# Reordering the first eight sequences of a gather-and-matmul kernel (ramp order on five queues)

## The chip, the cores and the metric

The kernel runs on one core of one Trainium2 chip. The metric is the device time of one execution in microseconds (us), the median of three runs.

## What is computed

64 sequences of 128 rows by 512 columns pass through two steps, each added to its input:

```python
attn_in = tanh(x @ W1 + b1); scores = attn_in @ v
p = softmax(where(mask_of_kind, scores, -1e30))      # prefix, postfix or cloze mask, one kind per sequence
x = x + (p @ x) / cnt
x = x + (x @ W[cat] + b[cat])                        # W[cat] is 512x512 float32, gathered per sequence
```

The kernel multiplies out the second step: with W' = W + identity it forms y = x W', and then out = y + p' y + b, where p' is p divided by cnt.

## The kernel before

Four sequences form a group g (16 groups). For each group one x tile of 1 MB is loaded and for each sequence k one W tile of 1 MB. In the steady part every float32 operand is split into a high and a low float32r half, and three products replace one float32 product. The work of one sequence is spread over the engines like this:

- SyncE (SP) issues nearly all loads and all stores. It runs through a list written by hand: the opening loads, then a loop over t with a store, now and then an x or a bias row, and the next W.
- VectorE (DVE) adds the identity to W (`add_identity`, 0.6 us), forms the low halves (`split_w_lo`, `split_xT_lo`, `split_z_lo`, `split_mix_lo`, `split_av_lo`), the row maxima (`max_group`) and every fourth output (`add_wide`).
- ScalarE (ACT) forms the high halves (`split_w_hi`, `split_xT_hi`, `split_z_hi`, `split_mix_hi`), tanh, exp, the scaling of the probabilities (`scale_group`) and three of four outputs (`copy_out`).
- GpSimd (POOL) adds the identity for two of four sequences and multiplies the row sums (`row_div`), and copies masks.
- TensorE (PE) runs `xw(k)` (12 products), `pz(k-2)` (3 or 4), and once per group `transpose_probs(g)`, `hidden(g+1)` (12) and `scores_group(g+1)` (2). Group 0 uses unsplit float32 (`xw_raw`, `hidden_raw`).

Every engine works strictly in the order of its program and waits on semaphores. From sequence 7 on (8 after the change) the order comes from loops. Before that, in the ramp, it is written out line by line, and the change touches this part. W buffers: 5 raw, 4 high, 3 low. `split_z_hi(3)` needs `pz(0)` done, since there are three z buffers. Below, w5 is the W tile of sequence 5, id5 its identity addition, x1 the x tile of group 1, T1 the transposes of group 1.

Of the kernel before, what the change touches and what calls it, by code (L numbers as in the profile page):

```python
# [38 lines left out]
def program(nc, xg, ids, w1, w, bias, out):  # L40
    GROUPS, P, DC, GS = xg.shape
# [14 lines left out]
    with ctx:  # L56
# [265 lines left out]
        def _(act):  # L322
# [70 lines left out]
            split_z_hi(1)
            split_w_hi(4)
            split_z_hi(2)
            split_mix_hi(0)
            tanh_group(1)
# [343 lines left out]
```

## Time and profile before

| | us |
|---|---|
| median of 3 runs | 311.19 (310.75 to 311.24) |
| profiled execution, its own time | 310.89 |
| its span | 308.9 |
| PE busy | 299.9 (97%) |
| DVE busy | 281.9 (91%) |
| ACT busy | 266.6 (86%) |
| POOL busy | 90.1 (29%) |

The page of the profile gives busy time by engine, a chain that ended last, and groups of instructions. The rows that matter here are single instructions of the first 61 us, in order of time, with what each had waited for.

### The profile page before, as it was taken

How to read it: one execution, taken by the hardware profiler on the slowest of the kernel's cores; microseconds unless marked ns; L12 is line 12 of the kernel's file. 1: busy time of each engine (PE TensorE's matmuls, PEld its weight loads, DVE VectorE, ACT ScalarE, POOL GpSimd, SP SyncE). 2: the span in 40 equal slices, each digit the busy share in tenths (PEclk: the TensorE clock that was granted, in tenths of full speed). 3: DMA queues.
4: the chain of work that ended last, by engine and by line, in shares of the span. 5: the costliest groups of instructions: out<-in, count | busy, mean ns of one | idle time of the engine just before them, and what ended most of it. 6: DMA issues, size and time to landing. Idle time of an engine off the chain costs nothing.

```text
span 308.9 us, 4918 instructions
## 1 busy us (share of the span) xinstructions
PE 299.9 (97%) x1292; PEld 233.8 (76%) x1292; DVE 281.9 (91%) x383; ACT 266.6 (86%) x431; POOL 90.1 (29%) x123
## 2 busy tenths in 40 slices
PE   7999899899999999999999999999999999999995
PEld 4444686688787878878788887878888787888884
DVE  4459889999999999999999999999999999999961
ACT  2287988989999998999999899998989999899952
POOL 4011612334142243414224341322434132302100
PEclk9999999999999999999999999999999999999999
DMA  7999999999999999999999999999999999997243
GB/s 265 366 426 366 421 412 423 371 344 326 360 372 332 396 313 405 356 356 375 337 404 300 407 363 363 365 337 398 311 405 355 353 380 308 413 333 228 66 135 137
DMA packets 23516, 105.69 MB, mean 342 GB/s; under 512 B 2625, under 2 KB 2626, under 8 KB 13378
## 3 DMA queue, kind: packets, MB, share of 16 engines
q1 hardware_dynamic: 23202, 104.08, 90.6%
q10 hardware_dynamic: 288, 1.31, 1.1%
q8 instruction: 10, 0.16, 0.2%
q14 instruction: 16, 0.13, 0.1%
HBM read 88.61 MB, written 16.78 MB: 341 GB/s over the span
## 4 chain that ended last, share of the span: by engine, by line
PE 82%; DMA 6%; issue 5%; DVE 3%; ACT 1%; POOL 1%; ACTq 0%; POOLq 0%; SPq 0%; DVEq 0%
PE ps_y L653 16%; PE ps_y L655 16%; PE ps_y L654 16%; PE ps_pre L615 12%; DMA w_raw<-in_L_cond_W 6%; PE ps_y L665 4%; PE ps_y L666 4%; PE ps_y L667 4%; PE ps_y L671 3%; PE ps_pT L632 2%; PE ps_y L641 1%; PE ps_scores L625 1%; PE ps_scores L623 1%; POOL w_raw L274 1%; DVE w_lo L465 1%
## 5 line engine op out<-in xcount | busy, mean ns | idle before, releaser
L465 DVE TENSOR_TENSOR w_lo<-w_raw,w_hi 128x2048 fp32r<-128x2048 f32 x60 | 140.1, 2335 | 0.0
L336 ACT ACTIVATE w_hi<-w_raw 128x2048 fp32r<-128x2048 f32 x60 | 115.5, 1924 | 8.9 <-POOL w_raw L274 7.5
L653 PE MATMUL ps_y<-w_hi,xT_hi 128*128 128x512 f32 x240 | 95.0, 396 | 0.0
L655 PE MATMUL ps_y<-w_hi,xT_lo 128*128 128x512 f32 x240 | 93.6, 390 | 0.0
L654 PE MATMUL ps_y<-w_lo,xT_hi 128*128 128x512 f32 x240 | 93.4, 389 | 0.0
L274 POOL TENSOR_TENSOR w_raw<-w_raw,ident 128x512 f32<-128x512 f32 x30 | 39.2, 1307 | 132.6 <-DVE w_lo L465 82.6
L655 PEld LDWEIGHTS ps_y<-w_hi,xT_lo 128*128 128x128 f32 x240 | 45.0, 188 | 9.8
L654 PEld LDWEIGHTS ps_y<-w_lo,xT_hi 128*128 128x128 f32 x240 | 45.1, 188 | 9.1
L653 PEld LDWEIGHTS ps_y<-w_hi,xT_hi 128*128 128x128 f32 x240 | 45.1, 188 | 8.9 <-issue 0.2
L493 DVE TENSOR_TENSOR z_lo<-ps_y,z_hi 128x512 fp32r<-128x512 f32 x64 | 43.5, 680 | 5.4 <-ACT z_hi L372 5.3
L372 ACT ACTIVATE z_hi<-ps_y 128x512 fp32r<-128x512 f32 x64 | 38.7, 604 | 7.8 <-PE ps_y L655 5.1
L281 POOL COPY mask<-penalty 128x128 bf16 x64 | 42.5, 695 | 9.8 <-issue 9.7
L458 DVE TENSOR_TENSOR xT_lo<-x_raw,xT_hi 128x2048 fp32r<-128x2048 f32 x15 | 34.2, 2281 | 0.0
L378 ACT ACTIVATE out_sb<-ps_y 128x512 f32<-128x512 f32 x48 | 28.9, 603 | 2.0 <-PE ps_y L671 2.0
L327 ACT ACTIVATE xT_hi<-x_raw 128x2048 fp32r<-128x2048 f32 x15 | 28.8, 1923 | 0.0
L453 DVE TENSOR_TENSOR w_raw<-w_raw,ident 128x512 f32<-128x512 f32 x33 | 22.5, 682 | 4.4 <-DMA w_raw<-in_L_cond_W 4.4
L665 PE MATMUL ps_y<-z_hi,mix_hi 128*128 128x512 f32 x64 | 25.2, 394 | 0.9 <-DVE z_lo L493 0.7
L666 PE MATMUL ps_y<-z_hi,mix_lo 128*128 128x512 f32 x64 | 24.9, 389 | 0.0
L667 PE MATMUL ps_y<-z_lo,mix_hi 128*128 128x512 f32 x64 | 24.9, 389 | 0.0
L351 ACT ACTIVATE probs<-ps_scores,neg_max 128x128 f32<-128x128 f32 x64 | 22.3, 359 | 2.0 <-DVE neg_max L478 2.0
L615 PE MATMUL ps_pre<-xT_hi,w_hi 128*128 128x512 f32 x56 | 22.9, 409 | 0.6 <-issue 0.6
L316 POOL TENSOR_TENSOR row_div<-row_sum,seen 128x4 f32<-128x4 f32 x16 | 6.4, 401 | 56.8 <-ACT probs L351 56.8
(70 smaller groups left out, 352.8 us busy)
## 6 DMA issues: line engine op xcount, KB each, us to landing
w_raw<-in_L_cond_W SPq DMA_DIRECT2D x63, 1024.0 KB, 8.6
out<-out_sb SPq DMA_DIRECT2D x64, 256.0 KB, 6.2
x_raw<-in_x SPq DMA_DIRECT2D x15, 1024.0 KB, 7.4
out_sb<-in_L_cond_b SPq DMA_DIRECT2D x16, 256.0 KB, 5.7
x_raw<-in_x SPq DMA_DIRECT2D x2, 512.0 KB, 4.8
w_raw<-in_L_cond_W ACTq DMA_DIRECT2D x1, 1024.0 KB, 6.1
w_pack<-in_W_b_v ACTq DMA_DIRECT2D x1, 257.0 KB, 2.9
b_raw<-in_L_cond_b SPq DMA_DIRECT2D x2, 128.0 KB, 12.9
```

The source lines that it names most:

```text
L274: nc.gpsimd.tensor_tensor(blocks, blocks, eye, ALU.add).then_inc(pool_wi_ready, 1)
L281: last = nc.gpsimd.tensor_copy(mask[g % 2][:, i:i + 1, :], penalty[:, bass.ds(kind, 1), :])
L336: nc.scalar.activation(w_hi[k % NH][:], w_raw[k % NW][:], ACT.Copy).then_inc(w_hi_ready, 1)
L372: nc.scalar.activation(z_hi[k % NZ][:], ps_y[k % NY][:], ACT.Copy).then_inc(z_hi_ready, 1)
L465: nc.vector.tensor_tensor(w_lo[k % NL][:], w_raw[k % NW][:], w_hi[k % NH][:].bitcast(F32), ALU.subtract).then_inc(w_lo_ready, 1)
L493: nc.vector.tensor_tensor(z_lo[k % NZ][:], ps_y[k % NY][:], z_hi[k % NZ][:].bitcast(F32), ALU.subtract).then_inc(z_lo_ready, 1)
L615: last = nc.tensor.matmul(ps_pre[:], wp[:, c, :], xp[g % NT][:, c, :], start=(c == 0 and i == 0), stop=(c == DC - 1 and i == 2))
L653: nc.tensor.matmul(y[:], xT_hi[q][:, c, xs], w_hi[k % NH][:, c, :], start=(c == 0), stop=False)
L654: nc.tensor.matmul(y[:], xT_hi[q][:, c, xs], w_lo[k % NL][:, c, :], start=False, stop=False)
L655: last = nc.tensor.matmul(y[:], xT_lo[q][:, c, xs], w_hi[k % NH][:, c, :], start=False, stop=(c == DC - 1))
L665: nc.tensor.matmul(y[:], mh, z_hi[k % NZ][:], start=False, stop=False, skip_group_check=True)
L666: nc.tensor.matmul(y[:], ml, z_hi[k % NZ][:], start=False, stop=False, skip_group_check=True)
```

## The change

- **Loads.** w1 moves from SP to ScalarE's queue, right behind w0. SP no longer waits for the second half of x0 but for w0 to land, then issues w2, w4, x1, w3, the bias table (two halves, `b_raw`), w5, x2, w6, a bias row, w7, w8, w9, x3. Before: w1, w2, x1, w4, w3, w5, bias table, x2, w6, bias row, w7, w8, and x3 only after the first store.
- **id3** is done by POOL, not DVE.
- **PE** runs the transposes of group 1 after `xw(5)` and `pz(3)`, not after `xw(4)` and `pz(2)`.
- **ACT and DVE** get another order for sequences 1 to 7, and the written-out part is one sequence longer.

```diff
-            return {3: 6, 4: 5}.get(k, k + 2 - pool_count(k - 1))
+            return k + 2 - pool_count(k - 1)
...
-            return k > G and k % G in (1, 2)
+            return k == 3 or k > G and k % G in (1, 2)
...
             sp.wait_ge(ids_in, 16)
-            sp.wait_ge(x0_in[1], 16)
-            load_w(1)
-            load_w(2)
+            cat_2 = load_cat(2)
+            sp.wait_ge(w_in[0], 16)
+            load_w(2, cat_2)
+            load_w(4)
             load_x(1)
-            load_w(4)
             load_w(3)
-            load_w(5)
             sp.dma_start(b_raw[0:C, :], bias).then_inc(b_low_in, 16)
             sp.dma_start(b_raw[C:P, :], bias).then_inc(b_high_in, 16)
+            load_w(5)
             load_x(2)
             load_w(6)
             load_wide(0)
+            load_w(7)
+            load_w(8)
+            load_w(9)
+            load_x(3)
...
             for g in range(GROUPS):
+                if g == 1:
+                    add_identity(3)
...
-            cat_0 = act.value_load(ids_row[0:1, 0:1], min_val=0, max_val=C - 1)
-            act.dma_start(w_raw[0][:], w[bass.ds(cat_0, 1)].rearrange("a p c h -> p (a c) h")).then_inc(w_in[0], 16)
+            for k in range(2):
+                cat = act.value_load(ids_row[0:1, k:k + 1], min_val=0, max_val=C - 1)
+                act.dma_start(w_raw[k][:], w[bass.ds(cat, 1)].rearrange("a p c h -> p (a c) h")).then_inc(w_in[k], 16)
...
-                if k < B and b == 0:
+                if k < B and (k == G + 1 or b == 0 and g >= 2):
                     transpose_probs(g)
```

First place: DVE from id4 (the second row of that kind here, `w_raw<-w_raw,ident`) to the maxima of group 1. Before:

```order
30 L484 RECIPROCAL row_scale<-row_div 128x4
31 L453 TENSOR_TENSOR w_raw<-w_raw,ident 128x4x128
32 L458 TENSOR_TENSOR xT_lo<-x_raw,xT_hi 128x2048
33 L453 TENSOR_TENSOR w_raw<-w_raw,ident 128x4x128
34 L465 TENSOR_TENSOR w_lo<-w_raw,w_hi 128x2048
35 L493 TENSOR_TENSOR z_lo<-ps_y,z_hi 128x512
36 L488 TENSOR_TENSOR mix_lo<-ps_pT,mix_hi 128x512
37 L470 SCALAR_TENSOR_TENSOR av_lo<-attn,w_pack,av_hi 128x512
38 L554 TENSOR_TENSOR b_both<-b_raw,b_both 64x512
39 L493 TENSOR_TENSOR z_lo<-ps_y,z_hi 128x512
```

The same stretch of the changed kernel (its lines are numbered otherwise):

```order
30 L502 RECIPROCAL row_scale<-row_div 128x4
31 L471 TENSOR_TENSOR w_raw<-w_raw,ident 128x4x128
32 L483 TENSOR_TENSOR w_lo<-w_raw,w_hi 128x2048
33 L506 TENSOR_TENSOR mix_lo<-ps_pT,mix_hi 128x512
34 L511 TENSOR_TENSOR z_lo<-ps_y,z_hi 128x512
35 L569 TENSOR_TENSOR b_both<-b_raw,b_both 64x512
36 L488 SCALAR_TENSOR_TENSOR av_lo<-attn,w_pack,av_hi 128x512
37 L476 TENSOR_TENSOR xT_lo<-x_raw,xT_hi 128x2048
38 L496 ISA ps_scores,neg_max<-ps_scores,mask 128x128
39 L496 ISA neg_max 128x1
```

The low half of x1 went from the front of the stretch to its end, behind av_lo of group 1; id3 is gone; z_lo of sequence 2 went behind the maxima.

Second place: ACT from the tanh of group 2 on. Before:

```order
35 L342 ACTIVATE attn<-ps_pre,w_pack 128x512
36 L344 ACTIVATE av_hi<-attn,w_pack 128x512
37 L378 ACTIVATE out_sb<-ps_y 128x512
38 L336 ACTIVATE w_hi<-w_raw 128x2048
39 L372 ACTIVATE z_hi<-ps_y 128x512
40 L336 ACTIVATE w_hi<-w_raw 128x2048
41 L351 ACTIVATE probs,row_sum<-ps_scores,neg_max 128x128 x4
42 L378 ACTIVATE out_sb<-ps_y 128x512
43 L372 ACTIVATE z_hi<-ps_y 128x512
44 L358 ACTIVATE probs<-probs,row_scale 128x128 x4
```

And in the changed kernel:

```order
39 L355 ACTIVATE attn<-ps_pre,w_pack 128x512
40 L357 ACTIVATE av_hi<-attn,w_pack 128x512
41 L391 ACTIVATE out_sb<-ps_y 128x512
42 L349 ACTIVATE w_hi<-w_raw 128x2048
43 L385 ACTIVATE z_hi<-ps_y 128x512
44 L391 ACTIVATE out_sb<-ps_y 128x512
45 L364 ACTIVATE probs,row_sum<-ps_scores,neg_max 128x128 x4
46 L349 ACTIVATE w_hi<-w_raw 128x2048
47 L385 ACTIVATE z_hi<-ps_y 128x512
48 L371 ACTIVATE probs<-probs,row_scale 128x128 x4
```

The high half of w10 (the second `w_hi` row) went behind the exp of group 2, between it and the scaling.

## Rows read from the trace of the kernel before

**Rows 1.** The page: the busy line of the engines.

```profile
PE 299.9 (97%) x1292; PEld 233.8 (76%) x1292; DVE 281.9 (91%) x383; ACT 266.6 (86%) x431; POOL 90.1 (29%) x123
```

**Rows 2.** Timeline, TensorE: start, length, engine, line, operation, waited before.

```profile
13.83 7.03 PE L641 MATMUL ps_y<-w_raw,x_raw 128*128 128x512 f32 x16
...
28.36 0.19 PEld L625 LDWEIGHTS ps_scores<-av_lo,ones 128*128 128x128 f32 x1 [0.59 <-DVE av_lo L470]
29.08 0.19 PEld L665 LDWEIGHTS ps_y<-z_hi,mix_hi 128*128 128x128 f32 x1 [0.54 <-DVE b_both L554]
...
35.79 0.66 PE L632 MATMUL ps_pT<-ident,probs 128*128 128x128 f32 x4 [1.19 <-ACT probs L358]
...
53.99 0.50 PE L665 MATMUL ps_y<-z_hi,mix_hi 128*128 128x512 f32 x1 [0.68 <-DVE z_lo L493]
...
55.99 0.66 PE L632 MATMUL ps_pT<-ident,probs 128*128 128x128 f32 x4 [0.80 <-ACT probs L358]
...
60.93 0.47 PE L615 MATMUL ps_pre<-xT_hi,w_hi 128*128 128x512 f32 x1 [0.62 <-issue]
```

**Rows 3.** Critical chain, in order of time: two later transposes, and two loads.

```profile
3.14 6.12 DMA w_raw<-in_L_cond_W
...
13.70 12.71 DMA w_raw<-in_L_cond_W
...
75.06 0.44 PE ps_pT L632 x4
...
93.19 0.44 PE ps_pT L632 x4
```

**Rows 4.** Timeline, VectorE: identities, low halves, and one reciprocal.

```profile
12.73 0.69 DVE L453 TENSOR_TENSOR w_raw<-w_raw,ident 128x512 f32<-128x512 f32 x1 [1.16 <-DMA w_raw<-in_L_cond_W]
...
20.28 0.69 DVE L453 TENSOR_TENSOR w_raw<-w_raw,ident 128x512 f32<-128x512 f32 x1 [3.05 <-DMA w_raw<-in_L_cond_W]
...
27.20 1.10 DVE L470 SCALAR_TENSOR_TENSOR av_lo<-attn,w_pack,av_hi 128x512 fp32r<-128x512 f32 x1
...
30.62 2.28 DVE L465 TENSOR_TENSOR w_lo<-w_raw,w_hi 128x2048 fp32r<-128x2048 f32 x1
34.24 0.18 DVE L484 RECIPROCAL row_scale<-row_div 128x4 f32<-128x4 f32 x1 [1.34 <-POOL row_div L316]
...
38.31 2.28 DVE L465 TENSOR_TENSOR w_lo<-w_raw,w_hi 128x2048 fp32r<-128x2048 f32 x1
...
45.71 0.87 DVE L470 SCALAR_TENSOR_TENSOR av_lo<-attn,w_pack,av_hi 128x512 fp32r<-128x512 f32 x1 [1.12 <-ACT av_hi L344]
...
47.10 3.07 DVE L465 TENSOR_TENSOR w_lo<-w_raw,w_hi 128x2048 fp32r<-128x2048 f32 x1
...
54.45 0.17 DVE L484 RECIPROCAL row_scale<-row_div 128x4 f32<-128x4 f32 x1
```

**Rows 5.** Timeline, GpSimd: its first three identities that met VectorE.

```profile
26.48 1.27 POOL L274 TENSOR_TENSOR w_raw<-w_raw,ident 128x512 f32<-128x512 f32 x1 [6.32 <-DMA w_raw<-in_L_cond_W]
32.32 1.73 POOL L274 TENSOR_TENSOR w_raw<-w_raw,ident 128x512 f32<-128x512 f32 x1 [4.57 <-DMA w_raw<-in_L_cond_W]
...
46.72 1.30 POOL L274 TENSOR_TENSOR w_raw<-w_raw,ident 128x512 f32<-128x512 f32 x1 [0.69 <-DMA w_raw<-in_L_cond_W]
```

**Rows 6.** DMA view: throughput in 40 slices of 0 to 62 us, then of 20 to 32 us.

```profile
GB/s 0 226 256 412 439 233 328 418 423 428 428 428 428 423 428 373 248 367 423 398 437 423 418 418 423 390 403 433 398 437 403 443 410 414 440 363 392 354 370 383
...
GB/s 410 437 437 410 410 437 410 437 437 410 437 410 437 437 273 341 191 328 225 273 259 294 300 382 355 437 437 410 410 437 437 382 437 410 437 437 280 376 539 410
```

**Rows 7.** Timeline, ScalarE: one high half, av_hi, the output after exp(2), scaling(2).

```profile
18.45 1.89 ACT L327 ACTIVATE xT_hi<-x_raw 128x2048 fp32r<-128x2048 f32 x1
...
25.49 0.72 ACT L344 ACTIVATE av_hi<-attn,w_pack 128x512 fp32r<-128x512 f32 x1
...
52.60 0.61 ACT L378 ACTIVATE out_sb<-ps_y 128x512 f32<-128x512 f32 x1
...
54.66 1.28 ACT L358 ACTIVATE probs<-probs,row_scale 128x128 f32<-128x128 f32 x4 [0.96 <-DVE row_scale L484]
```

More of the change, by code:

```diff
@@ L228, in load_wide @@
             def load_wide(g):
-                cat = sp.value_load(ids_row[0:1, G * g + WIDE:G * g + WIDE + 1], min_val=0, max_val=C - 1)
+                cat = load_cat(G * g + WIDE)
                 if g >= 1:
@@ L249, in _ @@
             load_wide(0)
-            for t in range(B + 3):
+            load_w(7)
+            load_w(8)
+            load_w(9)
+            load_x(3)
+            for t in range(3, B + 3):
                 g, b = t // G, t % G
-                if t >= 3:
-                    store(t - 3)
-                if b == 3 and g + 3 < GROUPS:
+                store(t - 3)
+                if b == 3 and 1 <= g < GROUPS - 3:
                     load_x(g + 3)
-                if b == 2 and 1 <= g < GROUPS:
+                if b == 2 and g < GROUPS:
                     load_wide(g)
@@ L391, in _ @@
             scale_group(0)
+            split_w_hi(4)
+            split_z_hi(1)
+            split_mix_hi(0)
             split_xT_hi(1)
[L393 to L397, printed above, removed]
             act.wait_ge(b_low_in, 16)
@@ L400, in _ @@
             nc.scalar.activation(b_both[:], b_raw[:], ACT.Copy).then_inc(b_hi_ready, 1)
+            tanh_group(1)
+            split_z_hi(2)
             split_w_hi(5)
+            split_z_hi(3)
             split_xT_hi(2)
+            copy_out(0)
             exp_group(1)
-            split_z_hi(3)
-            copy_out(0)
+            split_w_hi(6)
             scale_group(1)
-            split_w_hi(6)
+            split_z_hi(4)
+            split_w_hi(7)
             split_mix_hi(1)
-            split_z_hi(4)
+            split_z_hi(5)
             copy_out(2)
-            split_w_hi(7)
-            split_z_hi(5)
             split_w_hi(8)
@@ L416, in _ @@
             split_w_hi(9)
-            for k in range(G + 3, B + 3):
+            split_z_hi(6)
+            copy_out(4)
+            exp_group(2)
+            split_w_hi(10)
+            for k in range(2 * G, B + 3):
                 g, b = k // G, k % G
@@ L555, in _ @@
                 .then_inc(bias_ready, 1)
+            split_av_lo(1)
+            split_xT_lo(1)
+            max_group(1)
             split_z_lo(2)
-            max_group(1)
             split_w_lo(5)
+            split_z_lo(3)
+            split_xT_lo(2)
             row_scale_group(1)
-            split_xT_lo(2)
-            split_z_lo(3)
+            add_wide(0)
             add_identity(7)
-            add_wide(0)
             split_w_lo(6)
+            split_z_lo(4)
             split_mix_lo(1)
-            split_z_lo(4)
             add_identity(8)
@@ L571, in _ @@
             split_w_lo(8)
-            for k in range(G + 3, B + 1):
+            max_group(2)
+            split_w_lo(9)
+            row_scale_group(2)
+            split_z_lo(6)
+            add_identity(11)
+            for k in range(2 * G, B + 1):
                 g, b = k // G, k % G
@@ L638, in xw_raw @@
                         pe.wait_ge(wi_ready, c // HALF + 1)
+                    elif c == 0 and by_pool(k):
+                        pe.wait_ge(pool_wi_ready, pool_count(k))
                     elif k >= 1 and c == 0:
```

14 lines of the change are left out of this document (7 added, 7 removed).

## The prediction

> **What bounds the kernel now.** I read the page first. PE is busy for 97% of the span, DVE for 91%, and the page's chain lies on PE almost throughout [rows 1]. So ask where PE waits. The timeline of PE shows it waiting only in the first 61 us [rows 2]; after that the transposes come every 18.13 us (75.06, then 93.19) [rows 3] and nothing interrupts PE. The change ends at sequence 8, so its worth is the shift of the moment at which PE falls into that rhythm, which I read at the transposes of group 3, 75.06.
>
> PE's waits on the way are: low half of av 0.59 at 28.36, bias 0.54 at 29.08, T1 1.19 at 35.79, pz(6) 0.68 at 53.99, T2 0.80 at 55.99, hidden(3) 0.62 at 60.93 [rows 2]. That looks like 4.4 us to win. But every one of them ends with DVE's or ACT's work, and from 20.28 on DVE waits for others only 1.34 us at 34.24, 1.12 before the av_lo of group 2, and behind POOL (below) [rows 4]. DVE is the engine that is late. Whatever lets DVE start a long piece earlier is worth time; what only reorders PE is not.
>
> **The change part by part.**
>
> *w1 behind w0 on ACT's queue.* w0 lands at 3.14 + 6.12 = 9.26 [rows 3]. w1 landed at about 12.7, since its identity waited for it until 12.73 [rows 4]; the throughput falls to 233 and 328 GB/s between 7.8 and 10.9 us against some 425 around it [rows 6]. With w1 already queued, (425 - 233 + 425 - 328) x 1.55 us is 0.45 MB, or 1.05 us of the stream. But PE reaches xw(1) only at 13.83 and runs it and xw(2) without a gap [rows 2], so w1 early is worth nothing by itself. w2 is now issued after w0 has landed, 9.3, and should land 4.9 later, as w1 did after its issue at 7.8: 14.2. From there 1.05 MB at 425 GB/s is 2.5 us each.
>
> *Order of loads.* w4 comes at 16.7 (before: 20.2, where id4 waited for it [rows 4]), x1 at 19.2. From w4's landing to w6's at 32.2 the kernel before took 12.0 us for w3, w5, bias table, x2 and w6 [rows 4, 5]. At 2.5 each and 0.6 for the table that is 10.6. The rest went in a dip to 191 to 382 GB/s from 24.2 to 27.5 us [rows 6], which begins as the bias table moves. The same five loads follow x1 now. If the dip goes with the table, w6 lands at 19.2 + 12.0 = 31.2 and w5 two loads earlier, 26.2, against 26.41 before (13.70 + 12.71 [rows 3]); if not, 1.2 us or so earlier: 30.0 and 25.0. I take the dip as tied to the table, since it is the only one in the first 54 us. So of the stream's lead of 1.05 us, w5 keeps 0.2 and w6 1.0.
>
> *id3 to POOL.* DVE saves 0.6 us (0.69 in the row, of which the next operation overlaps some 0.08, as with all of DVE's here: 0.6 for an identity or a z, 2.2 for a w or xT low half [rows 4]). POOL is idle there; w3 lands at 21.7, id3 takes 1.3 [rows 5] and is done at 23.0, while PE is still in hidden_raw(1), whose tanh comes just ahead of av_hi at 25.49 [rows 7]. No cost for PE.
>
> *DVE, first place.* w_hi(4) now follows scale_group(0) at 18.45 (where xT_hi(1) stood [rows 7]), so w_lo(4) runs 20.35 to 22.55, then mix_lo(0) and z_lo(1) to 23.75. Now DVE waits: 0.65 for b_both (behind xT_hi(1), 21.9 to 23.7 on ACT, and 0.6 long), and, after its 0.6, 1.2 for av_hi(1). That one can't move: it starts at 25.49 + 0.76 = 26.25 [rows 7], fixed by PE's float32 products. So 1.9 us of DVE are lost here, which before held xT_lo(1).
> Then POOL. An identity on POOL and a DVE operation on two SBUF tiles don't run together: av_lo at 27.20 took 1.10 instead of 0.75 until just after id5's end at 27.75, w_lo at 47.10 took 3.07 instead of 2.28 while POOL's lasted to 48.02, and id6 at 32.32 took 1.73 instead of 1.27 behind the w_lo that ended at 32.90 [rows 4, 5]. Now id5 runs 26.3 to 27.5, so av_lo(1) ends at 28.0 instead of 27.0. xT_lo(1) takes 2.2 to 30.2, the maxima 1.0 to 31.2, z_lo(2) 0.6 to 31.8. w6 has landed at 31.2 and id6 runs until 32.5, so w_lo(5) ends at 34.65 (0.7 lost; before, id6 fell into a moment in which DVE had nothing to do). z_lo(3), xT_lo(2), row_scale, add_wide(0), id7: 0.6 + 2.2 + 0.1 + 0.6 + 0.6, and w_lo(6) starts at 38.75, against 38.31 [rows 4]. **+0.45.** The wait of 1.34 at 34.24 is gone, and so is id3, but 1.9 + 1.0 + 0.7 of new waits took their place.
>
> *T1 one sequence on.* PE: the waits at 28.36 and 29.08 fall away, since b_both and mix_lo(0) are early, and pz(0) starts some 0.6 sooner; xw(5) waits for w_lo(5) until 34.7, ends at 37.4, pz(3) at 38.4; scale_group(1) follows row_scale at 37.5 and ends at 38.8, so T1 waits only 0.4. PE has done more by then, but mix_hi(1) waits for T1 and ACT's w_hi(7), and id8 on DVE comes after mix_lo(1): w_lo(6) to 40.95, z_lo(4), mix_lo(1), id8 to 42.75, against 42.31. w_hi(8), tanh(2), av_lo, w_lo(8) and the maxima of group 2 then follow as before, av_lo waiting for av_hi as at 45.71 and w_lo(8) for POOL as at 47.10 [rows 4]. Nothing is gained or lost: still +0.45.
>
> *ACT, second place.* Before, exp(2) ended at 52.60; two short copies followed, and ACT waited 0.96 for row_scale(2), which came at 54.45 [rows 4, 7]. Now row_scale(2) comes 0.8 earlier, right behind w_lo(9), but w_hi(10) stands ahead of scale_group(2): exp to 53.05, w_hi(10) 1.8, z_hi(7) 0.5, scaling 1.2 (1.28 in the row [rows 7]), T2 at about 56.7 against 55.99. For DVE, row_div(2) (which waits for w_lo(9) on POOL, too), then z_lo(6) and id11, then w_lo(10) at 55.4 and xT_lo(3), which ends at about 61.6; hidden(3) waits for it: 0.3 to 0.4 more. **Together +0.8.** Bounds of this part: 0, if ACT's gap of 0.96 takes up most of w_hi(10), and 0.7 (T2's own shift).
>
> *Later loads* (w7, w8, w9, x3 before the first store): w8 still waits for xw(3), and w9 lands before its identity, which waits for w_lo(7). The first store waits for nothing new. I cost it at nothing: before, PE had no wait for a load there, and x3 comes earlier.
>
> Sum: 75.06 + 0.8. The profiled execution took 310.89, so 311.7; the median shown is 0.3 above it, 311.19, so 312.0. I take 311.9, since each lock of POOL and DVE was priced in full.
>
> **A rule beside the rows.** By the rows above two of those waits cost 1.7 us in the first place; without them the sum would be +0.8 - 1.7 = -0.9. The Trainium skill, page "SBUF — State Buffer", section "SBUF: two separate sides", says that DVE and GpSimd share a port pair by an exclusive lock, that a DVE operation with two SBUF inputs takes part in it, and that the loser blocks wholly. By that rule moving id3 to POOL gains only where DVE is not at such an operation, and the three rows agree with it.
>
> **The rivals.**
> - *No dip.* If the dip at 24 to 27 us was chance and doesn't follow the bias table, w5 lands at 25.0, before av_lo(1) is due, and w6 at 30.0, so id6 is done by 31.3. av_lo ends at 27.0, w_lo(6) starts at 37.5 (-0.8), and with the +0.4 of the second place, which stays, the shift is -0.4: 310.8. For it: a load of bias rows at 31 us made no such dip. Against it: the dip starts with the table's rows.
> - *The waits are won after all (the other side).* If POOL's identities cost DVE nothing, its pieces from 26.25 to w_lo(6) add up to 0.75 + 2.2 + 1.0 + 0.6 + 2.2 + 0.6 + 2.2 + 0.1 + 0.6 + 0.6 = 10.85, so w_lo(6) starts at 37.1, 1.2 early; and if row_scale(2) ahead of z_lo(6) gives back half of T2's wait of 0.80 [rows 2], another 0.4: 1.6 in all, 309.6 to 310.3. It decides from the point at which w5 has landed and been treated by POOL before 26.3 and w6 before 30.8. Against it: three rows of POOL against DVE [rows 4, 5].
> - *The stream is later.* w2 goes out after w0's landing, with nothing of SP's queued, and if the first packets are slow again or w5 comes after 26.7, av_lo, xT_lo(1) and w_lo(5) are pushed 0.5 further: +1.3 to +1.5, 312.5.
> - *Nothing at all.* The change takes a PE wait here and makes one there. Terms of +0.45 and +0.35, each good to some 0.3, may come to nothing: 311.2. This is the low end of the forecast case.
>
> **How the numbers follow.** Dip with the table (my forecast, own range +0.2 to +1.2): 0.5. No dip: 0.23. Won after all: 0.15. Later stream: 0.12. A difference under 0.2% (0.62 us) can't be told from none here. The forecast case splits into 0.29 slower and 0.21 same; no dip into 0.15 same and 0.08 faster; won is faster; later is slower. Faster 0.08 + 0.15 = 0.23; same 0.21 + 0.15 = 0.36; slower 0.29 + 0.12 = 0.41. Range: from the middle between "no dip" and "won", 310.2, to 312.8.
>
> **What would show it.** w1 landing by 11.8 and w2 by 14.3 in their waits; DVE idle about 1.9 us between 23.7 and 26.3; the second w_lo (w5's) of over 2.9 us; w_lo(6) at 38.5 to 39; T1 waiting under 0.5; T2 waiting 1 us behind w_hi(10); group 3's transposes at 75.6 to 76. The prediction is wrong if w5 lands before 25.3, or if DVE's slots behind POOL are short.

## The result, and the profile after

The changed kernel is slower: median 313.08 us (312.46 to 315.45, 11 runs) against 311.19 (310.67 to 312.95, 11 runs) of the kernel before, run beside it; ratio 1.0063, interval 1.0044 to 1.0082. That is 1.9 us, above the 311.9 that was forecast and above the range's upper end, 312.8. Repeated (after_again below) the ratio was 1.0044. The ratios here and below are those on record with their 95% intervals; they are not quotients of the two medians, and where the two differ enough to matter the text says so.

The page of the profiled execution: its span is 310.5 (before 308.9), and the busy line answers to [rows 1].

```profile
span 310.5 us, 4917 instructions
...
PE 301.8 (97%) x1292; PEld 234.2 (75%) x1292; DVE 282.9 (91%) x382; ACT 266.7 (86%) x431; POOL 93.2 (30%) x124
```

The chain that ended last, in order of time (start, length, what), over the ramp and the first regular groups:

```profile
13.20 11.39 DMA b_raw<-in_L_cond_b
24.72 0.49 issue
25.22 0.68 ACT attn L355
25.92 0.73 ACT av_hi L357
...
27.35 3.36 DVE xT_lo L476
...
57.48 0.66 PE ps_pT L654 x4
...
76.52 0.44 PE ps_pT L654 x4
...
94.67 0.44 PE ps_pT L654 x4
```

Group 3's transposes are at 76.52 instead of 75.06 [rows 3], 1.46 late, and the next come 18.15 later, as before. So the loss is made in the ramp. Where the chain before had the W tile of sequence 5 (13.70 12.71 [rows 3]) it now has the bias table: ScalarE forms b_both from it ahead of tanh of group 1, so tanh waits for the table, then comes av_hi, and behind that VectorE's low half of x1.

VectorE's timeline, the pieces that answer to [rows 4]:

```profile
17.61 0.69 DVE L471 TENSOR_TENSOR w_raw<-w_raw,ident 128x512 f32<-128x512 f32 x1 [0.42 <-DMA w_raw<-in_L_cond_W]
20.33 2.29 DVE L483 TENSOR_TENSOR w_lo<-w_raw,w_hi 128x2048 fp32r<-128x2048 f32 x1 [2.03 <-ACT w_hi L349]
...
25.34 0.69 DVE L569 TENSOR_TENSOR b_both<-b_raw,b_both 64x512 fp32r<-64x512 f32 x1 [1.52 <-ACT b_both L412]
26.68 0.75 DVE L488 SCALAR_TENSOR_TENSOR av_lo<-attn,w_pack,av_hi 128x512 fp32r<-128x512 f32 x1 [0.64 <-ACT av_hi L357]
27.35 3.36 DVE L476 TENSOR_TENSOR xT_lo<-x_raw,xT_hi 128x2048 fp32r<-128x2048 f32 x1
...
32.19 3.17 DVE L483 TENSOR_TENSOR w_lo<-w_raw,w_hi 128x2048 fp32r<-128x2048 f32 x1
...
38.08 0.17 DVE L502 RECIPROCAL row_scale<-row_div 128x4 f32<-128x4 f32 x1
...
39.34 2.28 DVE L483 TENSOR_TENSOR w_lo<-w_raw,w_hi 128x2048 fp32r<-128x2048 f32 x1
...
42.36 0.69 DVE L506 TENSOR_TENSOR mix_lo<-ps_pT,mix_hi 128x512 fp32r<-128x512 f32 x1
42.97 0.68 DVE L471 TENSOR_TENSOR w_raw<-w_raw,ident 128x512 f32<-128x512 f32 x1
...
54.67 0.18 DVE L502 RECIPROCAL row_scale<-row_div 128x4 f32<-128x4 f32 x1
...
55.95 2.38 DVE L483 TENSOR_TENSOR w_lo<-w_raw,w_hi 128x2048 fp32r<-128x2048 f32 x1
```

The wait of 3.05 for w4 is now 0.42, and the one of 1.34 for the row sums is gone. In their place stand 2.03, 1.52 and 0.64, and two low halves of 3.36 and 3.17 where 2.28 is the undisturbed length. GpSimd's timeline shows the identities that lie beside those two (26.93 and 31.91), and that both W tiles came later than forecast (26.2 and 31.2):

```profile
23.50 1.27 POOL L285 TENSOR_TENSOR w_raw<-w_raw,ident 128x512 f32<-128x512 f32 x1 [3.38 <-DMA w_raw<-in_L_cond_W]
26.93 1.63 POOL L285 TENSOR_TENSOR w_raw<-w_raw,ident 128x512 f32<-128x512 f32 x1 [2.16 <-DMA w_raw<-in_L_cond_W]
31.91 1.30 POOL L285 TENSOR_TENSOR w_raw<-w_raw,ident 128x512 f32<-128x512 f32 x1 [3.36 <-DMA w_raw<-in_L_cond_W]
...
54.06 0.58 POOL L329 TENSOR_TENSOR row_div<-row_sum,seen 128x4 f32<-128x4 f32 x1 [4.78 <-ACT probs L364]
```

ScalarE's timeline, b_both ahead of tanh, then the second place:

```profile
24.68 0.63 ACT L412 ACTIVATE b_both<-b_raw 128x512 fp32r<-128x512 f32 x1 [1.00 <-DMA b_raw<-in_L_cond_b]
25.22 0.67 ACT L355 ACTIVATE attn<-ps_pre,w_pack 128x512 f32<-128x512 f32 x1
25.92 0.72 ACT L357 ACTIVATE av_hi<-attn,w_pack 128x512 fp32r<-128x512 f32 x1
...
53.86 1.92 ACT L349 ACTIVATE w_hi<-w_raw 128x2048 fp32r<-128x2048 f32 x1
...
56.14 1.28 ACT L371 ACTIVATE probs<-probs,row_scale 128x128 f32<-128x128 f32 x4
```

And TensorE's waits, against [rows 2]:

```profile
30.85 0.47 PE L677 MATMUL ps_y<-w_hi,xT_hi 128*128 128x512 f32 x1 [0.26 <-DVE xT_lo L476]
35.50 0.47 PE L677 MATMUL ps_y<-w_hi,xT_hi 128*128 128x512 f32 x1 [0.74 <-DVE w_lo L483]
39.61 0.66 PE L654 MATMUL ps_pT<-ident,probs 128*128 128x128 f32 x4 [0.20 <-ACT probs L371]
...
55.48 0.50 PE L689 MATMUL ps_y<-z_hi,mix_hi 128*128 128x512 f32 x1 [0.93 <-DVE z_lo L511]
57.48 0.66 PE L654 MATMUL ps_pT<-ident,probs 128*128 128x128 f32 x4 [0.80 <-ACT probs L371]
62.42 0.47 PE L637 MATMUL ps_pre<-xT_hi,w_hi 128*128 128x512 f32 x1 [0.62 <-issue]
```

T1 hardly waits any more (0.20 for 1.19), yet it starts 3.8 us later: a sequence's products are ahead of it, as they should be, and with them a share of DVE's delay. Of the last three, pz(6) waits 0.93 for 0.68, T2 and hidden(3) as long as before, all of them 1.5 us later. These waits add up to less than those of [rows 2], so a list of TensorE's waits alone would not show the loss.

### The profile page after: what moved, and what is told of

It is laid out like the page before. It is cut to its first block, busy times and chain, and to the rows that moved or that the text cites. A ratio compares the mean times of both kernels' runs of the same rounds, so it can differ in the third digit from the quotient of the medians.

```text
span 310.5 us, 4917 instructions
## 1 busy us (share of the span) xinstructions
PE 301.8 (97%) x1292; PEld 234.2 (75%) x1292; DVE 282.9 (91%) x382; ACT 266.7 (86%) x431; POOL 93.2 (30%) x124
## 4 chain that ended last, share of the span: by engine, by line
PE 80%; DMA 6%; DVE 4%; issue 4%; ACT 4%; SPq 1%; ACTq 0%; DVEq 0%
PE ps_y L677 16%; PE ps_y L679 16%; PE ps_y L678 16%; PE ps_pre L637 12%; PE ps_y L689 4%; PE ps_y L690 4%; PE ps_y L691 4%; DMA b_raw<-in_L_cond_b 4%; PE ps_y L695 3%; PE ps_pT L654 2%; DMA w_raw<-in_L_cond_W 2%; DVE xT_lo L476 2%; DVE w_lo L483 1%; PE ps_scores L647 1%; PE ps_scores L645 1%
## 5 line engine op out<-in xcount | busy, mean ns | idle before, releaser
L285 POOL TENSOR_TENSOR w_raw<-w_raw,ident 128x512 f32<-128x512 f32 x31 | 40.5, 1307 | 130.2 <-DVE w_lo L483 82.2
L292 POOL COPY mask<-penalty 128x128 bf16 x64 | 43.8, 714 | 8.9 <-issue 8.8
L476 DVE TENSOR_TENSOR xT_lo<-x_raw,xT_hi 128x2048 fp32r<-128x2048 f32 x15 | 35.3, 2355 | 0.0
L371 ACT ACTIVATE probs<-probs,row_scale 128x128 f32<-128x128 f32 x64 | 20.7, 419 | 2.4 <-DVE row_scale L502 2.4
```

The lines of the kernel that those rows point to most:

```text
L285: nc.gpsimd.tensor_tensor(blocks, blocks, eye, ALU.add).then_inc(pool_wi_ready, 1)
L292: last = nc.gpsimd.tensor_copy(mask[g % 2][:, i:i + 1, :], penalty[:, bass.ds(kind, 1), :])
L476: nc.vector.tensor_tensor(xT_lo[g % NT][:], x_raw[g % NX][:], xT_hi[g % NT][:].bitcast(F32), ALU.subtract).then_inc(xT_lo_ready, 1)
```

## The experiments

Where an experiment's profile is read, T0 and T3 are the starts of the transposes of group 0 and group 3. Before they are 20.70 and 74.90, 54.20 apart; in the changed kernel 20.65 and 76.36, 55.71 apart, and in its repetition 54.73. (75.06 and 76.52 in the chain are within the same transposes, 0.16 behind their starts.) One profile's distance thus carries about 1 us of chance; the ratios of repeated runs decide.

The start of w_lo(6) on VectorE shows where that chance lies. From T0 to w_lo(6) the three profiles have 17.61, 18.69 and, in the repetition, 17.71: its T0 came 0.74 us later (21.39), while id5 ran 0.26 earlier (26.67), so the loads behind w0 did not move with T0. From w_lo(6) to T3 it is 36.59 before, 37.02 in the changed kernel and 37.02 again in its repetition. This second part is steady: 36.91 to 37.06 in the six variants of the changed kernel whose clock didn't fall (a1, a2, a4, c1, c2, d3), 36.32 to 36.73 in those of the kernel before. So of the 1.46 us, 1.03 lie ahead of w_lo(6) and 0.43 behind it.

**The changed kernel once more** (after_again), to have it beside the others.

> The changed kernel itself beside the others, to have its size on this chip: all theories expect the ratio of the first measurement again, 1.006, and the transposes of group 3 some 55.7 to 55.9 us after those of group 0.

312.61 us, ratio 1.0044 (1.0025 to 1.0063). The loss holds, at 1.0 us between the medians and 1.4 by the ratio.

### Parts taken back from the changed kernel

**tanh(1) ahead of b_both**, and on VectorE av_lo ahead of it:

```diff
             split_xT_hi(1)
+            tanh_group(1)
             act.wait_ge(b_low_in, 16)
             act.wait_ge(b_high_in, 16)
             nc.scalar.activation(b_both[:], b_raw[:], ACT.Copy).then_inc(b_hi_ready, 1)
-            tanh_group(1)
```

> The changed kernel (313.1 us median) with tanh(1) ahead of b_both on ScalarE and av_lo(1) ahead of the bias low half on VectorE. Theory A (b_both waited for the bias table until 24.68 and pushed tanh(1) from 24.77 to 25.22, av_lo(1) by 0.43): tanh(1) back at 24.8, av_lo(1) at 26.25; since POOL's id5 then blocks xT_lo(1) from 26.9 to 28.2 all the same, only 0.3 us comes back: 312.8. Theory B (the loss is in the late stream alone, w5 landing at 26.9): no change, 313.1. Theory C (the loss is T1's place on TensorE): no change.

312.79 us, ratio 1.0003 (0.9985 to 1.0020). The kernel before was at 312.36 beside this run and the next three, above its 311.2 to 311.6 everywhere else, and the changed kernel itself was not run there. So these four ratios don't say how much of the loss came back; the four are better compared with each other. The profile: VectorE waits for av_hi for 2.38 instead of for b_both and av_hi, and b_both, now beside GpSimd's identity, takes 1.65 instead of 0.69. T3 minus T0 is 55.72, w_lo(6) starts 18.66 after T0 (18.69 in the changed kernel). The wait changed its name.

**The bias table in one transfer** to 128 partitions (the table is given twice in DRAM):

```diff
-            sp.dma_start(b_raw[0:C, :], bias).then_inc(b_low_in, 16)
-            sp.dma_start(b_raw[C:P, :], bias).then_inc(b_high_in, 16)
+            sp.dma_start(b_raw[:], bias[0:P, :]).then_inc(b_low_in, 16)
```

> The changed kernel with the bias table loaded by one transfer into 128 partitions (the table stands twice in DRAM) instead of two into 64 each. Theory A (the dip in throughput comes from two transfers that each reach half of the partitions): no dip at 21 to 24 us, table at 23, w5 lands 1.2 us sooner at 25.7, w_lo(6) starts at 38.5 instead of 39.34, T3 0.9 to 1.2 sooner: 312.0. Rival (the dip comes from reading 64 rows of 2 KB in any shape, or by chance at that time): dip stays, 313.1.

311.92 us, ratio 0.9995 (0.9974 to 1.0016), T3 minus T0 55.04. The dip in throughput at the table was gone, w5 came 0.6 us earlier than in the changed kernel, w_lo(6) started at 38.75, 0.6 earlier too. The median is 0.8 to 1.2 us below those of the three other variants run beside it (312.79, 313.13, 312.70), which all keep the table in two transfers. So in the changed kernel the two transfers may well cost some of the loss. But the DMA view of this kernel (40 slices of 18 to 38 us) has another dip, at 29 to 31:

```profile
GB/s 475 344 475 344 492 459 287 455 442 430 467 360 492 426 377 459 426 410 459 344 508 459 279 209 168 311 430 401 430 426 426 393 459 377 459 442 410 426 459 393
```

**id3 back on VectorE**, behind z_lo(1):

```diff
-            return k == 3 or k > G and k % G in (1, 2)
+            return k > G and k % G in (1, 2)
...
             split_z_lo(1)
+            add_identity(3)
             dve.wait_ge(b_hi_ready, 1)
```

> The changed kernel with id3 back on VectorE, behind z_lo(1) at 23.7, where VectorE waits 1.5 us for b_both. Theory A (that wait hides it): 0 to +0.1 us, 313.1 to 313.2. Rival (VectorE is short of time everywhere in the ramp, so each 0.6 us of work counts): +0.6, 313.7.

313.13 us, ratio 1.0020 (1.0001 to 1.0039). In its profile TensorE's granted clock fell to 0.50 of full for some 3 us at 59 us (below), so its T3 isn't read. Up to w_lo(6) it is the changed kernel: VectorE had nothing to do where id3 went, and xT_lo(1) and w_lo(5) took 3.36 and 3.13, and w_lo(6) starts 18.93 after T0 for 18.69. Where id3 is done made no difference that shows.

**w_hi(10) ahead of exp(2)**, as in the kernel before:

```diff
-            copy_out(4)
-            exp_group(2)
             split_w_hi(10)
+            exp_group(2)
+            copy_out(4)
```

> The changed kernel with w_hi(10) ahead of exp(2) again, as in the kernel before. Theory A (w_hi(10) behind exp(2) cost 0.2 of T2, whose shift grew from 1.25 at w_lo(8) to 1.49): T2 at 57.2 instead of 57.48, 312.8. Rival (the second place cost 0.35 or more, as predicted): 312.7 or less; or nothing, if row_scale(2) is the limit: 313.1.

312.70 us, ratio 1.0012 (0.9990 to 1.0034). T2 doesn't wait any more, but hidden(3) does, for 1.64 instead of 0.62:

```profile
56.86 0.60 PE L654 MATMUL ps_pT<-ident,probs 128*128 128x128 f32 x4
62.77 0.47 PE L637 MATMUL ps_pre<-xT_hi,w_hi 128*128 128x512 f32 x1 [1.64 <-issue]
```

T2's wait of 0.8 was given back at hidden(3), which reads xT_lo(3), and from w_lo(6) to T3 it is 37.04, as in the changed kernel: at the second place VectorE's xT_lo(3) decides, not ScalarE's order.

**x1 ahead of w4 again** (loads, high and low halves):

```diff
-            load_w(4)
             load_x(1)
+            load_w(4)
...
-            split_w_hi(4)
+            split_xT_hi(1)
             split_z_hi(1)
+            split_w_hi(4)
             split_mix_hi(0)
-            split_xT_hi(1)
...
             add_identity(4)
+            split_xT_lo(1)
             split_w_lo(4)
```

> The changed kernel with x1 loaded ahead of w4 again, and both halves of x1 split ahead of w4's, where VectorE is otherwise idle. Theory A (the change lost its time by moving 2.2 us of VectorE work, xT_lo(1), out of an idle stretch into the busy one behind av_lo(1)): w_lo(6) at 37.9 instead of 39.3, group 3's transposes 1.0 to 1.4 us sooner counted from those of group 0, ratio to before 1.000 to 1.002. Rival (the loss is T1's place, id3 and the order at exp(2)): no change, 1.0045 to 1.006.

312.07 us, ratio 1.0030 (1.0001 to 1.0059); in its profile T3 minus T0 is 54.15, that of the kernel before. By the ratio half of the loss may be left, by the profile nothing: w_lo(6) starts 17.13 after T0, 0.5 less than before, which makes up for the 0.43 behind it. Here w_lo(4) meets id3 and takes 3.34, and id6, begun together with w_lo(5) (30.88), takes 3.44.

**id5 and id6 on VectorE** (and `by_pool`, the rule that says whose identity it is, with them):

```diff
             split_av_lo(1)
+            add_identity(5)
             split_xT_lo(1)
             max_group(1)
             split_z_lo(2)
+            add_identity(6)
             split_w_lo(5)
```

> The changed kernel with id5 and id6 on VectorE (1.2 us more work there, none on GpSimd between 24 and 43 us). Theory A (VectorE and GpSimd exclude each other, and each of GpSimd's two identities costs VectorE 0.7 to 1.1 us): w_lo(5) takes 2.3 instead of 2.9 to 3.2 us, xT_lo(1) or av_lo(1) isn't stretched, w_lo(6) starts at 38.5 to 39.2, the time is the same or 0.3 to 0.8 less, 1.002 to 1.005. Rival (the long operations had another reason): they stay long and 1.2 us of work comes on top, 1.010.

312.06 us, ratio 1.0027 (1.0006 to 1.0049). VectorE's timeline shows both low halves at their own length, each 0.6 of an identity later:

```profile
28.06 2.29 DVE L476 TENSOR_TENSOR xT_lo<-x_raw,xT_hi 128x2048 fp32r<-128x2048 f32 x1
...
32.72 2.29 DVE L483 TENSOR_TENSOR w_lo<-w_raw,w_hi 128x2048 fp32r<-128x2048 f32 x1
...
39.05 2.28 DVE L483 TENSOR_TENSOR w_lo<-w_raw,w_hi 128x2048 fp32r<-128x2048 f32 x1
```

The 1.08 and 0.89 were GpSimd's identities. Against them stands 1.2 of work and waits for the tiles, so only 0.3 of w_lo(6)'s delay came back.

**One table and tanh(1) first together:** the edits of the first and second experiment.

> The changed kernel with the bias table in one transfer and tanh(1) ahead of b_both. Theory A (the table's late landing and the dip are 0.5 to 0.9 us of the loss, the order of xT_lo(1) is the rest): 1.001 to 1.003. Rival (the dip is most of it): 0.999 or less.

312.27 us, ratio 1.0027 (1.0005 to 1.0048). w_lo(6) starts at 38.82. Both together still leave it above the kernel before.

**Three things taken back together:** x1 ahead of w4, id5 and id6 on VectorE, tanh(1) and av_lo(1) ahead of b_both; T1, ScalarE's second place, id3, w1 and the table's position stay as changed.

> The changed kernel with three things taken back together: x1 ahead of w4 (loads, high and low half), identities 5 and 6 by VectorE instead of GpSimd, and tanh of group 1 and the low half of av ahead of b_both. Theory A, the first place holds most of the loss: from group 0's transposes to group 3's 54.3 us, ratio to before 1.000 to 1.001. Theory B, the loss sits in the second place (high half of w10 behind the exp of group 2), in T1 and in the later loads: 55.2 us, ratio 1.003.

312.09 us, ratio 1.0009 (0.9991 to 1.0028). By the ratio the loss is gone to within the interval, which still allows 0.9 us; the medians are 0.68 us apart (312.09 and 311.41), and the single profile keeps 1.11 (T3 minus T0 55.31), 0.79 of it ahead of w_lo(6) and 0.32 behind. So it isn't shown that these three parts are the whole loss. A row shows a wait that this kernel makes itself: id3 on GpSimd now begins just after w_lo(4) (23.43), and TensorE waits for it.

```profile
23.55 3.30 POOL L285 TENSOR_TENSOR w_raw<-w_raw,ident 128x512 f32<-128x512 f32 x1 [2.56 <-DMA w_raw<-in_L_cond_W]
```

```profile
26.91 3.70 PE L667 MATMUL ps_y<-w_raw,x_raw 128*128 128x512 f32 x8 [1.40 <-POOL w_raw L285]
```

### Parts put into the kernel before

**One table:** the same edit of the table alone.

> The kernel before with the bias table loaded by one transfer into 128 partitions. Theory A (two 64-partition transfers make the dip, and b_both and w_hi(5) wait for what lands late): no dip at 24 to 27 us, b_both and w5 sooner by 1 us or more, 0.4 to 0.8 us less than before in the end, a ratio of 0.998. Rival (the ramp is bound by VectorE's work, which is the same): no change, 1.000.

311.45 us, ratio 0.9984 (0.9962 to 1.0007). This excludes neither of the two theories; in the kernel before, one transfer makes no difference that can be told from none.

**w1 on ScalarE's queue:**

```diff
-            sp.wait_ge(x0_in[1], 16)
-            load_w(1)
+            sp.wait_ge(w_in[0], 16)
...
-            cat_0 = act.value_load(ids_row[0:1, 0:1], min_val=0, max_val=C - 1)
...
+            for k in range(2):
+                cat = act.value_load(ids_row[0:1, k:k + 1], min_val=0, max_val=C - 1)
```

> The kernel before with w1 on ScalarE's queue and w2 issued once w0 has landed, the order of loads else kept. Theory A (the stream is 0.4 to 1.0 us ahead, and id5, id6 and w_hi(5) are bound by it): 0.3 to 0.8 us less, 0.998. Rival (the earlier identities only move into VectorE's long operations): 0 to +0.3.

311.20 us, ratio 0.9992 (0.9976 to 1.0008), T3 minus T0 54.25. Nothing, as forecast for w1 by itself.

**T1 one sequence later:**

```diff
-                if k < B and b == 0:
+                if k < B and (k == G + 1 or b == 0 and g >= 2):
```

> The kernel before with the transposes of group 1 one sequence later and nothing else. Theory A (TensorE isn't what is late; mix_hi(1) and mix_lo(1) come later than ScalarE's and VectorE's programs reach them, so both wait): T1 waits for nothing, but the transposes of group 3 come 0.5 to 1.5 us later, 1.002 to 1.005. Rival (TensorE's wait of 1.19 us at T1 is given back in part): 0.3 to 1.0 us less.

311.18 us, ratio 0.9993 (0.9973 to 1.0012). Nothing, as the prediction forecast for this part; both theories written down for this run missed. Its T1 waits for nothing. T3 minus T0 is 55.10, but of these 0.90 more, 0.77 lie ahead of w_lo(6), where id4 was already 0.72 later (21.00 for 20.28), long before T1, and 0.13 behind it.

**w1 on ScalarE's queue and one table:** both edits.

> The kernel before with w1 on ScalarE's queue, w2 issued once w0 has landed, and the bias table in one transfer. Theory A (ScalarE's w_hi(5) waits for b_both and w5, both sooner by 1 us or more; the two gains add up): w_lo(6) at 37.5, group 3's transposes 0.5 to 1.0 us sooner, 0.997. Rival (as with either alone, 0.998 and 0.999, no difference that can be measured): 0.998 to 1.000.

310.99 us, ratio 0.9986 (0.9959 to 1.0013). Its profile is the quickest of all (span 308.1), but the runs don't set it apart from the kernel before.

**w4 ahead of x1, alone:**

```diff
-            load_x(1)
             load_w(4)
+            load_x(1)
...
-            split_xT_hi(1)
+            split_w_hi(4)
             split_z_hi(1)
-            split_w_hi(4)
+            split_xT_hi(1)
...
             add_identity(4)
-            split_xT_lo(1)
             add_identity(3)
             split_w_lo(4)
...
+            split_xT_lo(1)
             split_z_lo(2)
```

> The kernel before with only this of the change: w4 loaded ahead of x1, its high half ahead of x1's, and the low half of x1 on VectorE behind av_lo and b_both of group 1. Theory A, this order is the main cost, since it empties VectorE while it waits for av_hi(1): w_lo(6) starts at 39.3 instead of 38.3, group 0's to group 3's transposes 55.2 us, ratio 1.003. Theory B, the order is free and the bias table's place is what costs: 54.2 us, ratio 1.000.

313.10 us, ratio 1.0058 (1.0034 to 1.0083), T3 minus T0 56.56. Put into the kernel before, this one part costs as much as the whole change. Two things in its profile don't belong to the order of w4 and x1 as the changed kernel has it. id3 stands ahead of w_lo(4) on VectorE and waited 4.88 us for w3; the next kernel takes that away. And T1, at its old place, waits 2.09 for ScalarE, after which the granted clock falls (windows: stretch and its length, TensorE's busy time, weight loads, VectorE, ScalarE, GpSimd, granted clock, DMA share, GB/s):

```profile
38.00:39.00 1.00, 0.10 (x1) 0.10 (x2) 1.00 (x1) 1.00 (x4) 1.00 (x1) 1.00 1.00 418
39.00:40.00 1.00, 1.00 (x7) 0.92 (x8) 1.00 (x2) 1.00 (x1) 1.00 (x2) 1.00 0.96 397
40.00:41.00 1.00, 1.00 (x5) 0.76 (x4) 1.00 (x3) 1.00 (x2) 0.34 (x2) 0.55 1.03 412
41.00:42.00 1.00, 1.00 (x4) 0.81 (x3) 1.00 (x2) 1.00 (x4) 0.00 (x0) 0.50 1.08 436
```

It is at 0.50, the lower of its two levels (1.2 for 2.4 GHz), until 43.5 or so (0.74 from 43 to 44, then 1.00). In 8 of this kernel's 12 runs the mean clock was 0.995 or less, and their median is 313.7; the other four have 312.7, 1.3 us above the kernel before.

**w4 ahead of x1, with id3 on GpSimd:**

```diff
-            return k > G and k % G in (1, 2)
+            return k == 3 or k > G and k % G in (1, 2)
```

> The kernel before with w4 loaded ahead of x1 and split in that order (as d4_w4_first), but with the identity of sequence 3 on GpSimd, as in the changed kernel. d4 had VectorE wait 4.9 us for w3 in front of w_lo(4). Theory A, the order itself costs, whoever adds the identity: w_lo(4) starts early, but VectorE has nothing to do until av_hi of group 1 and xT_lo(1) still comes behind it: ratio 1.003 to 1.005. Theory B, d4's loss was VectorE's wait for w3 behind id4: ratio 1.000 to 1.001.

313.22 us, ratio 1.0066 (1.0042 to 1.0090). VectorE's timeline, w_lo(4), what it waited for after, the low half of x1 behind it, w_lo(5) and w_lo(6):

```profile
22.36 2.29 DVE L467 TENSOR_TENSOR w_lo<-w_raw,w_hi 128x2048 fp32r<-128x2048 f32 x1 [1.98 <-ACT w_hi L338]
...
27.52 0.75 DVE L472 SCALAR_TENSOR_TENSOR av_lo<-attn,w_pack,av_hi 128x512 fp32r<-128x512 f32 x1 [1.21 <-ACT av_hi L346]
29.84 0.69 DVE L554 TENSOR_TENSOR b_both<-b_raw,b_both 64x512 fp32r<-64x512 f32 x1 [1.57 <-ACT b_both L402]
30.56 2.29 DVE L460 TENSOR_TENSOR xT_lo<-x_raw,xT_hi 128x2048 fp32r<-128x2048 f32 x1
...
34.32 3.11 DVE L467 TENSOR_TENSOR w_lo<-w_raw,w_hi 128x2048 fp32r<-128x2048 f32 x1
...
41.60 2.28 DVE L467 TENSOR_TENSOR w_lo<-w_raw,w_hi 128x2048 fp32r<-128x2048 f32 x1
```

The wait for w3 is gone and the loss stayed. T1 waits 2.17 here too, and the clock fell in five of the ten runs; the other five, at 0.998 or more, have a median of 313.14, 1.6 above the kernel before. w_lo(6) starts 19.63 after T0 (21.97); before it was 38.31 - 20.70 = 17.61. VectorE waits for nothing between b_both at 29.84 and w_lo(6), and the clock fell only behind T1 at 39.06, so the clock had no part in these 2.0 us. The order costs by itself, whoever adds the identity, and the early T1 on top of it brings the fall of the clock. One thing is not as in the changed kernel: the table still comes behind w5 here, and the 1.57 for b_both stands ahead of xT_lo(1) on top of the 1.21 for av_hi. So d4 and e1 show that the order costs, not how much of it the changed kernel pays.

**id3 on GpSimd, w1 on ScalarE's queue, one table, and the order of before:** the edits above together.

> The kernel before with three things that each looked harmless or better: w1 on ScalarE's queue behind w0, the bias table in one transfer to 128 partitions (table given twice in DRAM), and the identity of sequence 3 on GpSimd. It keeps the order of x1 and w4, T1 and ScalarE's and VectorE's order. Theory A, VectorE is late in this stretch and 0.6 us of work taken from it comes through: 0.5 to 0.9 us faster, ratio 0.997. Theory B, the waits behind it (for av_hi of group 1 at 1.3 us, for the row sums) take it up: ratio 0.9986 as without it, or nothing.

311.71 us, ratio 0.9996 (0.9974 to 1.0017). Taking 0.6 us from VectorE gained nothing, and GpSimd's and TensorE's timelines say why: id3 begins just after w_lo(4) (22.87 to 25.15), an operation on two SBUF tiles, is not done until 26.3 or so (the row holds two identities, id3's and w5's), and TensorE waits 1.64 for it.

```profile
23.07 4.44 POOL L272 TENSOR_TENSOR w_raw<-w_raw,ident 128x512 f32<-128x512 f32 x2 [2.94 <-DMA w_raw<-in_L_cond_W]
```

```profile
26.34 3.70 PE L642 MATMUL ps_y<-w_raw,x_raw 128*128 128x512 f32 x8 [1.64 <-POOL w_raw L272]
```

### What makes the dip in throughput

Over any 2 us (four slices) of 18 to 28 us, all 14 kernels with the table in two transfers fell to between 210 and 328 GB/s as it moved, and the 6 with one transfer never below 388. But five of those six fell to between 234 and 262 at the bias row of sequence 3 (256 KB, one DRAM row to all partitions), where the other fourteen stayed above 340. Two kernels take the two apart. The first reads the halves from different rows:

```diff
-            sp.dma_start(b_raw[0:C, :], bias).then_inc(b_low_in, 16)
-            sp.dma_start(b_raw[C:P, :], bias).then_inc(b_high_in, 16)
+            sp.dma_start(b_raw[0:C, :], bias[0:C, :]).then_inc(b_low_in, 16)
+            sp.dma_start(b_raw[C:P, :], bias[C:P, :]).then_inc(b_high_in, 16)
```

> The kernel before, with the bias table given twice in DRAM and its two halves read from different rows (both transfers still write 64 partitions each). Theory A, two transfers to half the partitions cause the dip: throughput falls to under 300 GB/s for some 3 us as the table moves, as in every run with two halves. Theory B, reading rows a second time causes it (the second half rereads the 64 rows of the first; in the runs with one transfer the dip came at the bias row of group 0, 31 us, to 140 to 280 GB/s): no dip at the table, one at the bias row.

The dip stays at the table (slices of 18 to 38 us; 356 to 266 from 25.5 to 29), so rereading the same rows is not its cause. Its one execution took 313.1 us; T0 was at 22.51.

```profile
GB/s 426 459 426 393 442 426 442 393 442 442 410 410 426 475 377 356 275 299 266 315 320 315 393 426 393 426 442 410 352 459 430 393 414 442 410 426 426 410 426 410
```

The second has the table in one transfer and loads 128 different rows where the bias row of sequence 3 belongs (so it leaves out that bias):

```diff
+                if g == 0:
+                    sp.dma_start(out_sb[WIDE][:], bias[0:P, :]).then_inc(wide_in, 16)
+                    return
```

> The kernel before with the table in one transfer, and the bias row of group 0 replaced by 128 different rows (so the outputs of sequence 3 are not the reference's). Theory A, half partitions, has nothing to say on the dip at 31 us that the runs with one transfer showed: it stays if it belongs to that transfer's place. Theory B, rows read a second time: the dip stays, since these rows too were read before. Theory C, 128 packets from one row: the dip at 31 us goes, and throughput stays above 350 GB/s from 24 to 34 us.

Now neither dip is there (same slices), though these rows had been read before too; its one execution took 310.52 us.

```profile
GB/s 328 459 426 410 475 377 426 492 328 459 459 360 344 455 471 352 442 508 328 475 344 459 508 279 397 438 459 459 360 492 328 459 508 328 475 328 459 524 311 475
```

So there are two causes: two transfers to 64 partitions each, and one row read for all partitions. The first is shown by 14 kernels against 6 and by the first of these two; for the second it is one kernel against five. Why the row makes a dip only where the table made none stays open. The kernel before has the dip at the table as well, and taking it away there changed nothing that can be told from none (b1, c4). In the changed kernel it may cost: a2 is 0.8 us or more below the kernels beside it, and c3, with one transfer and tanh ahead, is at 1.0027 where the repetition is at 1.0044.

The Trainium skill, page "SBUF — State Buffer", section "Door 1: The DMA port swizzle", ties a transfer's bandwidth to how many of the 16 ports its partitions reach, and by its formula partitions 0 to 63 reach only half of them. The runs agree in so far as the dip came with the two half-partition transfers (210 to 328 GB/s) and not with the one over all partitions (388 or more). That the 1 MB loads around them slow as well is more than the section says.

## Why the prediction was wrong

The direction was right and the size too small: a shift of 0.8 was forecast, 1.46 was measured at group 3's transposes and 1.9 between the medians (1.4 by the ratio of the repetition). Neither of the prediction's two signs of being wrong came: w5 didn't land before 25.3, and VectorE's slots behind POOL weren't short. By the prediction's own steps:

- **DVE, first place: +0.45. This is the step that failed, by its size.** w_lo(6) started at 39.34, 1.03 late, not 38.75. The mechanism stands as described: VectorE stood still for 2.16 us between the end of z_lo(1) at 23.82 and av_lo(1) at 26.68, and xT_lo(1) and w_lo(5) fell onto id5 and id6. Two sizes in it were too small. "That one can't move: it starts at 25.49 + 0.76 = 26.25" was wrong: b_both stands ahead of tanh(1) on ScalarE, the table landed only at 24.6, so av_hi started at 25.92 and av_lo at 26.68, 0.43 late; I had put b_both at 23.7, behind xT_hi(1), without asking when its table lands. The waits were 1.52 + 0.64 = 2.16 for 1.9, 0.26 more. And the two low halves took 3.36 - 2.28 + 3.17 - 2.28 = 1.97 more, for the 1.7 priced, 0.27 more, as w5 and w6 came 0.7 late (26.93 and 31.91 for 26.2 and 31.2).
- **That the order of w4 and x1 costs** is shown in the kernel before: alone it costs 0.58 and 0.66% (d4, e1; 0.4 and 0.5% in the runs without the clock's fall). In the changed kernel it is shown in part. The order alone, GpSimd's identities alone, and table and tanh together, each taken back in runs beside each other (c1, c2, c3), left 0.27 to 0.30% with intervals that nearly reach zero; order, identities and tanh together are at 1.0009, with 0.68 us left between the medians (d3). How the loss divides among order, lock and table is not settled.
- **T1 one sequence on: nothing.** Right by itself (b3). In the changed kernel mix_lo(1) started at 42.36, 0.22 after z_lo(4) made room, since ScalarE's mix_hi(1) stands behind w_hi(7) and ended at 42.33, so id8 was 1.26 late where w_lo(6) had been 1.03. My "still +0.45" missed this. Its wait was 0.20 for 0.4. d4 and e1, with T1 at its old place, wait 2.1 us there: the move saves the changed kernel part of what the order costs, which is argued from these two profiles alone.
- **ACT, second place: +0.35.** The shift grew by 0.23 there (id8 to T2: 1.26 to 1.49), but not for the reason given: with w_hi(10) ahead of exp(2) again (a4) T2 came sooner and T3 did not. VectorE's rows account for it: row_scale(2), now right behind w_lo(9), comes only at 54.67, since its row_div on GpSimd ended at 54.64, which is 0.16 lost, and w_lo(10) takes 2.38 for 2.29. With the 0.2 at mix_lo(1) that is about the 0.43 behind w_lo(6). This is read from rows; no run takes row_scale(2) alone back.
- **w1: nothing by itself.** Right (b2). **id3 to POOL: no cost.** Right in the changed kernel, where it fell into VectorE's idle time (1.27 long), and for that reason only: with the order of before it takes about 3.3 us and TensorE waits 1.4 to 1.6 (d3, e2). I had costed it by GpSimd's idle time and not asked what VectorE does beside it.
- **Order of loads, dip tied to the table.** The dip came with the table, 21 to 24.5 us, in the changed kernel and in its repetition. w5 and w6 were later than forecast by 0.7, and the fault lies ahead of w4: id4 ran at 17.61, not 16.7. From there to id6 it took 14.3 us, for the 14.5 (2.5 and the old 12.0) that I had put.
- **What would show it.** Right: VectorE idle about 1.9 (2.16), w5's w_lo over 2.9 (3.17), T1 under 0.5 (0.20). Out of bounds: w_lo(6) at 38.5 to 39 (39.34), T2 at 56.7 (57.48), group 3 at 75.6 to 76 (76.52). T2 waited 0.80, for about 1. The identities of sequences 1 and 2 ran at 12.16 and 14.95 without waiting, so these rows don't tell whether w1 and w2 landed by 11.8 and 14.3.
- **The rivals.** "The stream is later", with a chance of 0.12, fits best: its condition, w5 after 26.7, held (26.93), and its shift of 1.3 to 1.5 is that of T3 (1.46), though it was the table and not w5 that pushed av_lo. Its 312.5 is still 0.6 below the median, though the profiled execution took 312.46.
- **Slips without effect on the sum.** The row of hidden(3)'s wait names "issue" as what ended it, not DVE or ACT. And the dip at the table isn't the only one in the first 54 us: the 233 and 328 GB/s from 7.8 us, which the prediction itself prices, stand in the same view.

## What to carry to other kernels

On an engine that is late, price an order not by the length of its pieces but by what it can do while it waits: x1's low half was worth its place ahead of av_lo because it filled time in which the changed kernel's VectorE stood still for 2.16 us. Ask of every instruction ahead of a critical one when its own data lands, small tables too. And in these traces identities on GpSimd cost VectorE nothing only beside its idle time or an operation with an input in PSUM (z_lo kept its 0.68 at 47.75, beside an identity of 1.31 from 47.97), so moving one means looking at both timelines in that very stretch.
